# Scan stage of a hybrid layer: row normalisation on ScalarE in two passes, and VectorE's work of a chunk in another order

## What is computed

```
xn  = (x - mean(x)) / sqrt(var(x) + 1e-5)          # over the last axis, 256 values
Bu_r, Bu_i = xn @ (dt*B_real).T, xn @ (dt*B_imag).T
s_t = Lbar * s_(t-1) + Bu_t                         # complex, over the 1024 steps of a batch row
y   = Re(s) @ C_real.T - Im(s) @ C_imag.T + D*xn
x1  = x + y @ W_out.T + b_out
```

## Time and profile before

| | before |
|---|---|
| device time, median of 3 runs | 3928.14 us (3921.84 to 3932.45) |
| span of the profiled execution | 3930.1 us |
| first block of the scan stage | up to about 34 us of the span |
| slots of the scan stage | about 39 us to 378 us |
| TensorE, weight load, VectorE, ScalarE, GpSimd busy over the span | 93%, 60%, 75%, 57%, 42% |

### The profile page before, as it was taken

How to read it: one execution, slowest core, us unless ns; L and a number is a source line. 1 busy time by engine, 2 the same in 40 slices (tenths; PEclk the granted TensorE clock), 3 DMA queues, 4 the chain that set the end, 5 groups by cost and what they waited for, 6 DMA issues and landing times. The chain is left out here.

```text
span 3930.1 us, 77952 instructions
## 1 busy us (share of the span) xinstructions
PE 3667.3 (93%) x26062; PEld 2353.8 (60%) x26062; DVE 2960.1 (75%) x9275; ACT 2237.0 (57%) x4407; POOL 1663.9 (42%) x2027
## 2 busy tenths in 40 slices
PE   6998999998689999999999999999999997999997
PEld 5887766665445555555555555555555554666664
DVE  8998577675677788788778878878877884576675
ACT  1100565555166666666666666666666665556654
POOL 2332132333445555554555545556455520132323
PEclk9999999999699999999999999999999998999999
DMA  2333122111877776877768777687876752121211
GB/s 71 102 101 103 43 65 65 46 57 35 158 112 114 112 117 107 121 109 115 123 108 116 117 112 118 105 126 104 117 122 110 101 71 61 34 69 60 65 39 49
DMA packets 701469, 361.31 MB, mean 92 GB/s; under 512 B 305072, under 2 KB 668080, under 8 KB 701104
## 3 DMA queue, kind: packets, MB, share of 16 engines
q1 hardware_dynamic: 701104, 356.65, 50.8%
HBM read 204.49 MB, written 150.99 MB: 90 GB/s over the span
## 5 line engine op out<-in xcount | busy, mean ns | idle before, releaser
L1839 ACT ACTIVATE att_probs<-att_s 128x512 f32<-128x512 f32 (+1 forms) x2560 | 1319.3, 557 | 755.3 <-PE att_s L1928 430.9
L1719 DVE CUSTOM_DVE_ANT_0 att_s<-att_s,att_above 128x384 f32<-128x384 f32 (+3 forms) x2048 | 958.0, 514 | 189.0 <-PE att_s L1958 188.9
L1980 PE MATMUL att_s<-att_qs,att_ks 49*128 49x512 f32 (+3 forms) x3072 | 917.9, 388 | 90.0 <-ACT att_probs L1839 29.1
L1958 PE MATMUL att_s<-att_ks,att_qs 48*128 48x512 f32 (+3 forms) x3072 | 964.2, 407 | 5.8 <-DVE att_maxima L1722 3.7
L1980 PEld LDWEIGHTS att_s<-att_qs,att_ks 49*128 49x128 f32 x3072 | 459.7, 185 | 650.9 <-ACT att_probs L1839 433.6
L1722 DVE TENSOR_REDUCE att_maxima<-att_s 128x1 f32<-128x512 f32 x1024 | 668.8, 682 | 225.6 <-PE att_s L1958 219.3
L2008 PE MATMUL att_o_ps<-att_probs,att_vs 128*32 128x512 f32 (+3 forms) x6144 | 632.1, 499 | 0.5 <-ACT att_probs L1839 0.5
L1958 PEld LDWEIGHTS att_s<-att_ks,att_qs 48*128 48x128 f32 x3072 | 487.6, 188 | 25.1 <-DVE att_maxima L1719 8.0
L1097 PE MATMUL ffn_h2p<-ffn_h,ffn_w 128*128 128x512 f32 x768 | 363.3, 595 | 3.0 <-ACT ffn_h L968 0.9
L1928 PE MATMUL att_s<-att_mask,att_places 64*128 64x64 bf16 (+1 forms) x3072 | 332.5, 205 | 0.0
L1719 DVE DVE_READ_ACCUMULATOR2_ANT att_maxima<- 128x1 f32 x2048 | 290.0, 142 | 0.0
(11 more groups left out here) (292 smaller groups left out, 6331.1 us busy)
## 6 DMA issues: line engine op xcount, KB each, us to landing
att_staged<-qk_scratch SPq DMA_DIRECT2D x768, 128.0 KB, 7.5
qk_scratch<-att_parts SPq DMA_DIRECT2D x128, 512.0 KB, 3.7
ffn_x<-x SPq DMA_DIRECT2D x64, 512.0 KB, 5.2
ssm_x<-in_L_attn_a_x_dram SPq DMA_DIRECT2D x32, 512.0 KB, 3.8
x<-ssm_y SPq DMA_DIRECT2D x32, 512.0 KB, 3.0
x<-ffn_y SPq DMA_DIRECT2D x32, 512.0 KB, 2.9
att_x<-x SPq DMA_DIRECT2D x32, 512.0 KB, 12.3
v_scratch<-att_v_tok SPq DMA_DIRECT2D x32, 512.0 KB, 3.4
```

The costliest lines, as they stand in the source:

```text
L1719: last = v.tensor_tensor_reduce(scores, scores, above[:, CH - w:CH], 1.0, -3.0e38, ALU.add, ALU.max, to)
L1839: a(probs[u % 2][2 * g + p][:, 0:n], bank[:, 0:n], ACT.Exp).then_inc(exp_done, 1)
L1958: last = mm(bank[:, col:col + w], rows_of(qs[buf], g, KROWS, p, BT * blk, BT * (blk + 1)), rows_of(ks[buf], g, KROWS, p, t0, t1), start=k ...
L1980: last = mm(bank[:, col:col + w], rows_of(ks[buf], g, SHIFT + 1, p, BT * j, BT * (j + 1)), rows_of(qs[buf], g, SHIFT + 1, p, t0, t1), star ...
```

## The change

`center_and_scale` on ScalarE takes the place of `scale` on VectorE for chunks 1 to 31: a first pass of four instructions adds the negated mean (`ACT.Identity` with a bias column), a second pass of four multiplies by rstd (`ACT.Copy` with a scale column), in place in `xn`. GpSimd computes the negated mean with one more 128x4 instruction in `rstds`. Chunk 0 keeps `scale` on VectorE. In VectorE's slot `normalise(n+2)` moves from behind `low(n+1)` to ahead of it. TensorE's and SyncE's lists are as before.

```diff
         def rstds(pool, n, k, old):
             pool.wait_ge(moments_done, n + 1)
+            if old:
+                pool.wait_ge(xn_ready, n - 1)
+            nc.gpsimd.tensor_tensor(minus_mean[k][:, :], moments[k][:, :, 0], minus_one[:, :], ALU.mult).then_inc(mean_negated, 1)
             nc.gpsimd.tensor_tensor(var_eps[k][:, :], moments[k][:, :, 1], eps[:, :], ALU.add).then_inc(eps_added, 1)
             pool.wait_ge(eps_added, n + 1)
-            if old:
-                pool.wait_ge(xn_ready, n - 1)
             nc.gpsimd.tensor_tensor(rstd[k][:, :], var_eps[k][:, :], minus_half[:, :], ALU.pow).then_inc(rstd_ready, 1)
...
             if old:
+                dve.wait_ge(mean_negated, n - 1)
                 dve.wait_ge(eps_added, n - 1)
             dve.wait_ge(stats_done, n + 1)
...
-        def scale(dve, n, k, old):
+        def center_and_scale(act, n, k, old):
+            act.wait_ge(mean_negated, n + 1)
+            if old:
+                act.wait_ge(turned, KT * (n - 1))
+            for t in range(TT):
+                last = nc.scalar.activation(xn[k][:, t, :], xt[k][:, t, :], ACT.Identity, bias=minus_mean[k][:, t:t + 1])
+            last.then_inc(centered, 1)
+            act.wait_ge(centered, n)
+            act.wait_ge(rstd_ready, n + 1)
+            for t in range(TT):
+                last = nc.scalar.activation(xn[k][:, t, :], xn[k][:, t, :], ACT.Copy, scale=rstd[k][:, t:t + 1])
+            last.then_inc(xn_ready, 1)
+
+        def scale(dve, n, k):
             dve.wait_ge(rstd_ready, n + 1)
-            if old:
-                dve.wait_ge(turned, KT * (n - 1))
...
                 normalise(dve, 1, 0, 1, False)
-                scale(dve, 1, 1, False)
                 scan(0, 0, False)
 
-
                 def slot(n, it, k, old, more):
-                    low(dve, n + 1, 1 - k)
                     if more:
                         normalise(dve, n + 2, it + 1, k, True)
+                    low(dve, n + 1, 1 - k)
                     scan(n + 1, 1 - k, old or k == 1)
-                    if more:
-                        scale(dve, n + 2, k, True)
                     residual(n, it, k, old)
...
             @block.scalar
             def _(act):
-                evacuate(act, 1, 1, False)
-                with act.Fori(1, n_steps) as it:
+                center_and_scale(act, 1, 1, False)
+
+                def slot(n, k, old, more):
+                    evacuate(act, n + 1, 1 - k, old or k == 1)
+                    if more:
+                        center_and_scale(act, n + 2, k, True)
+
+                slot(0, 0, False, True)
+                slot(1, 1, False, True)
+                with act.Fori(1, n_steps - 1) as it:
                     for k in range(2):
-                        evacuate(act, 2 * it + k, k, True)
+                        slot(2 * it + k, k, True, True)
+                slot(2 * (n_steps - 1), 0, True, False)
```

More of the change, by code:

```diff
@@ L99, in ssm_phase @@
         var_eps = [sb(f"var_eps{k}", [P, TT]) for k in range(2)]
+        minus_mean = [sb(f"minus_mean{k}", [P, TT]) for k in range(2)]
         carrier = sb("carrier", [1, 1])
-        minus_half, eps = sb("minus_half", [P, TT]), sb("eps", [P, TT])
+        minus_half, eps, minus_one = sb("minus_half", [P, TT]), sb("eps", [P, TT]), sb("minus_one", [P, TT])
         u_cos, u_sin, u = sb("u_cos", [P, CH]), sb("u_sin", [P, CH]), sb("u", [P, CH])
@@ L109, in ssm_phase @@
         y_stored = [sem(f"ssm_y_stored{k}") for k in range(2)]
-        (stats_done, moments_done, eps_added, rstd_ready, xn_ready, turned, xnT_ready, xnT_lo_ready, bu_ready, u_parts, u_ready,
+        (stats_done, moments_done, mean_negated, eps_added, rstd_ready, centered, xn_ready, turned, xnT_ready, xnT_lo_ready, bu_ready, u_parts, u_ready,
          w_ready, w_turned, out_ready, xb_ready, y_ready, const_ready) = [sem("ssm_" + n) for n in (
-             "stats_done", "moments_done", "eps_added", "rstd_ready", "xn_ready", "turned", "xnT_ready", "xnT_lo_ready", "bu_ready",
+             "stats_done", "moments_done", "mean_negated", "eps_added", "rstd_ready", "centered", "xn_ready", "turned", "xnT_ready", "xnT_lo_ready", "bu_ready",
              "u_parts", "u_ready", "w_ready", "w_turned", "out_ready", "xb_ready", "y_ready", "const_ready")]
@@ L226, in _ @@
                     nc.gpsimd.memset(minus_half[:, :], -0.5).then_inc(const_ready, 1)
+                    nc.gpsimd.memset(minus_one[:, :], -1.0).then_inc(const_ready, 1)
                     step(nc.gpsimd.memset(euler[:, :], float(np.e)))
@@ L238, in _ @@
                     pool.wait_ge(decay_ready, 1)
-                    pool.wait_ge(const_ready, 2)
+                    pool.wait_ge(const_ready, 3)
                     rstds(pool, 0, 0, False)
@@ L279, in _ @@
                     v.tensor_scalar(cl_sin[:, :, N:P], cst[:, :, 0, :], -1.0, None, ALU.mult).then_inc(weights_step, 1)
-                    scale(dve, 0, 0, False)
+                    scale(dve, 0, 0)
                     def fraction(dst, src):
```

## The result

| | before | after |
|---|---|---|
| device time, median of 8 runs each | 3930.95 us (3921.84 to 3947.27) | 3953.19 us (3946.31 to 3958.41) |
| ratio to before, 95% interval | | 1.0054 (1.0042 to 1.0065) |
| span of the profiled execution | 3930.1 us | 3956.1 us |

The kernel is slower by 0.54%, some 21 to 22 us. It was forecast at 3954 us in a range of 3941 to 3966. The increase that was forecast, 25.7 us, stood on 3928.14 us, the median of three runs of the kernel before; over the eight runs here that median is 3930.95. So the increase came out 3.5 us smaller than forecast, and it is luck that the time itself lies within 1 us of 3954.

What follows compares the result with a forecast made beforehand. TensorE was taken to bound the kernel, with VectorE waiting for it once a slot. The terms 0 + 25.5 + 0.2 + 0 + 0 gave +25.7 us, a median of about 3954 us, range 3941 to 3966.

Steps and rivals of the forecast that it cites:

- Rival A: In the slots, VectorE sets the pace, so the 1.38 us of `scale` count in 30 slots: 3887 us; chance 4%.
- Part 1: In the slots, `scale` leaves VectorE, which only waits longer for the same `out`: 0 us.
- Part 2: In slots 2 to 29, `normalise` ahead of `low` makes `out` start 0.91 us later a slot: 25.5 us.
- Part 3: In the first slots, turn(2)'s wait goes and `low` comes later: 0.2 us lost after two slots.
- Parts 4 and 5: ScalarE's eight instructions a chunk and GpSimd's extra product stay hidden: 0 us, `xn` ready 1.7 to 4 us early.
- Rival C: ScalarE is late with `xn`; at 1.1 us an instruction the turn waits 1.5 us a slot more: about 4000 us; 3%.
- Rival B: The slack for `low` is larger than the rows say, loss under 0.42 us a slot: 3930 to 3940 us; 7%.
- Rival D: The clock falls in each projection as TensorE stands still: 81 us more, about 4035 us; chance 3%.
- The signs: Profile after: `y` to `y` 11.3 to 11.5 us, `xnT_lo` wait 0.6 to 0.8, VectorE idle 1.5 to 2.2, clock 1.00.

Runs made afterwards that it cites:

- ScalarE's part alone: The change without its new order: rows normalised on ScalarE, `low` again ahead of `normalise`; 3925.35 us against 3930.70 before.
- order alone: The kernel before with only `normalise(n+2)` moved ahead of `low(n+1)`, `scale` still on VectorE; 3952.82 us, ratio 1.0069.
- chunk 1 on ScalarE: The kernel before with only the rows of chunk 1 normalised on ScalarE; 3917.30 us against 3921.15.
- the turn inside `out`: The change with `turn(n+2)` ahead of the last matmuls of `out(n)`, ScalarE copies freed earlier, `low(n+2)` ahead of `residual(n)`; 3905.05 us against 3921.15 before.
- four stats ahead: The change with all four `bn_stats` of `normalise(n+2)` ahead of `low(n+1)` and the `bn_aggr` behind it; 3939.97 us, 1.0030 to before.
- the turn inside out and `scale` on VectorE: As the turn inside `out`, but with the rows scaled on VectorE as before the change; 3946.86 us, 1.0060 to before.

## Why the prediction was right

**What bounds the stage** was read rightly: TensorE, with VectorE waiting for it. Rival A (VectorE sets the pace, 3887 us) falls with the kernel that has ScalarE's part alone: VectorE is relieved of 1.4 us a slot and the slot goes from 10.50 to 10.45.

**Part 1, `scale` leaves VectorE, taken as 0.** In the old order it gave 0.05 us a slot, 1.3 us in 28: close, but not zero. In every second slot before, the wait behind the turn was 0.33 us; with ScalarE's part alone it is 0.25 in the slots that I read. The 0.33 stands in every second slot also where `scale` stayed on VectorE with one other thing changed (order alone, chunk 1 on ScalarE), so it goes with `scale` there; by what path was not tested. In the new order the part gives nothing: the slot is 11.29 us in the change and in the kernel with the order alone, since TensorE waits for `low` later in the slot. There the 0 was right.

**Part 2, `normalise` ahead of `low`, taken as 0.91 us a slot, 25.5 us.** Its mechanism and place are shown by the order alone and by the row of kernels with 0 to 1.7 us ahead of `low`. The size was 0.79 (22.2 us in 28 slots), both for the change against before and for the order alone against before; between the two kernels with the rows on ScalarE it is 11.29 - 10.45 = 0.84. In a slot of the kind that the prediction read, with `y` 0.20 us behind the turn, `out` starts 227.97 - 223.03 = 4.94 us behind E and not 5.05. The 0.63 us behind `low` held to the hundredth (214.85 + 1.25 to 216.73). What was 0.11 too large was VectorE's way there: `normalise` took 214.85 - 213.13 = 1.72 us to the start of `low`, not the 1.80 it took to the start of `scan`, and `low` 1.25, not 1.28.

**Part 3, the first slots, taken as +0.2.** y(1) came at -0.2. In it a gain and a loss nearly cancel, as in the working: ScalarE's part alone moved y(1) by -2.5, the order alone by +3.2 (they do not simply add, since the waits of the start overlap). The difference of 0.4 us to the sum was there before the first slot ended: `project(0)` ended earlier, and `scan(0)` started at 39.02 us and not at 39.50, the case of a faster projection that the prediction had named beside its sum (timeline of DVE, after).

```profile
39.02 0.69 DVE L423 TENSOR_TENSOR ssm_u_cos<-ssm_bu,ssm_cos 128x512 f32<-128x512 f32 x1 [3.16 <-PE ssm_bu L494]
```

Turn(1) waited 1.09 us for ScalarE, which was in the working's doubt, not in its sum; it cost nothing, since `out(0)` stood behind `low(1)`.

**Parts 4 and 5, ScalarE and GpSimd, taken as 0** with 1.7 to 4 us in hand: 3.65 us in hand in the slots, and no turn there waits for `xn`. Rival C falls. The instruction's price lay between the ends that the rows gave, at 495 ns for either pass (median of 124, after). The Trainium skill (ScalarE: Activation LUTs, What ACT_TABLE_LOAD costs) gives 280 ns + 0.833 ns an element for an instruction with a column as bias, an estimate of 493 ns for 256 elements, and the trace agrees. Four take 1.71 us, which is 0.405 from start to start.

**Rival B** (a larger slack than the rows say) falls with the threshold: two `bn_stats` are free and four are not. **Rival D** (the clock) falls with the 1.00 of the slots, with a wait of 0.47 us in each.

**The signs.** VectorE's idle time ahead of `y`, the `xn` rows and the clock came as named. Two signs fell a little short: the slot is 11.29 us on the average, where 11.3 to 11.5 was named, and the wait on `xnT_lo` shows as 0.47 and 0.39 us by turns, where 0.6 to 0.8 was. By the starts the delay is whole: `out` comes 4.94 us behind the turn, where it was 4.14.

The sum, 25.7 us, was 3.7 above the 22.0 that the stage grew by; 3.3 of it is the 0.12 us a slot by which part 2 was too large, and 0.4 the start. The median grew by 22.2 us.

## What to carry to other kernels

Where two engines are nearly full, find in the timeline of one period who waits for whom; relief for the engine that waits comes out as idle time in front of its next wait, as it did here (1.7 us ahead of each `y`). When an operation is moved in a list, take the distance from the end of what it now delays to the moment it is wanted: the part of the move within that slack is free, and the rest counted whole in every period here. And an offload that is worth nothing can be what another order needs: with the turn inside `out` the ScalarE passes were worth 1.4 us a slot, without it 0.05 or nothing.

## What the runs showed that was not expected

- A matmul that had to wait for `xnT_lo` takes longer to the next start: 0.34 us and not 0.23 for 512 columns at a granted clock of 1.00, also for the second pair, where the timeline shows no idle time (216.16 to 216.50). Only the second pair counts for `out`, since it starts 0.06 us behind the end of `low` whatever the first pair took. So of the 0.8 us a slot 0.11 come from this and 0.06 from that start.
- The granted clock fell to about half at 43 to 46 us in both profiles of the kernel before, behind waits of 1.65 and 1.81 us, and again (0.50 at 46 to 47 us) behind one of 2.40 us in the kernel with four stats ahead, but not behind one of 2.58 us in the kernel after. Ahead of turn(1) it fell behind a wait of 1.65 us with the turn inside out and `scale` on VectorE (0.50 at 43 to 46 us), and stayed at 1.00 behind one of 1.59 us with chunk 1 on ScalarE. In the kernel before it cost nothing, since TensorE would have waited for `low` instead; what sets it stays open.
- `out`, 32 matmuls, took 6.30 us to the next turn before and after the change alike, with VectorE busy 94% or 77% of the time and with ScalarE's work beside it.
